# Keeping half of a hidden layer and computing the other half twice: a graph layer with a mixture of experts on one Trainium2 core

## Chip, cores and metric

One core of a Trainium2 chip runs the whole program. The metric is the device time of one execution, in microseconds. All times are of single launches; the profile is of one further launch.

## What is computed

The reference takes node features `x` (6250 nodes, 256 channels), normalizes them, runs two graph convolutions with batch norms over 100,000 edges and adds the result to `x`. Then comes the part that matters here, a feed-forward layer with 8 experts and top-1 routing:

```python
xf = layernorm(x)                                   # 6250 x 256
H = gelu(xf @ W1 + b1)                              # 6250 x 1024
probs = softmax(H @ Wg + bg); assign = argmax(probs)
for e in range(8):
    y = H @ Wd[e] + bd[e]                           # 6250 x 256
    out += where(assign == e, probs[:, e] * y, 0)
return x + out
```

Only the expert that `assign` names counts for a node, so the kernel sorts the nodes by expert and multiplies each tile of 128 sorted nodes with one expert's `Wd`.

## The kernel before

Activations and weights are split in two float16 halves, a high and a low one, and a product is made of three matmuls: high x high, low weight x high, high weight x low. The hidden layer has 1024 units, that is `KH` = 8 chunks of 128. Nodes are taken in tiles of 128 and pairs of tiles of 256. All five engines run one instruction list each, ordered by semaphores; nothing is scheduled automatically. A `Block` ends when all engines have come to its end.

The stages are: `prepare`, the first `aggregate`, `linear1`, `linear2`, the second `aggregate`, `finish_gnn`, and then the two that the change touches.

*The gate stage* (`gate`, 25 pairs in the order of the nodes). GpSimd copies the rows of a pair to `stage`; TensorE transposes them with four fp32 matmuls into bank `TBANK` (`pe_transpose`, L1873); ScalarE (`act_xt`, L1896) and VectorE (`dve_xt`, L1928) make the high and low halves `xt_hi`, `xt_lo`. `pe_hidden` then does 8 chunks of 6 matmuls (L1886), 256 columns each, into four PSUM banks in turn. For each chunk ScalarE takes the Gelu into `hf` (L1913) and, for five of eight, scales it to the high half (L1908); VectorE does the other three (`DVE_HIGH`, L1940) and all low halves (L1945). So `h16` holds the halves of all 8 chunks with the hidden units on the partitions. They are used twice. Once by `logits` on TensorE (L2085), which gives 8 gate logits per node; VectorE's `choose` and TensorE's and VectorE's `ranks` and `place` find the expert and the slot of each node in the order by expert, a few pairs behind. And once by the experts, through DRAM: SP waits for all 8 chunks of a pair (L2022), turns `h16` with one crossbar DMA transpose into rows of 2048 halves per node (`turned`, a ring of `HRING` = 6, L2026), and GpSimd scatters these rows by slot to `sorted_h` (L2068) beside the node's own row in `sorted_rows` (L2062). ScalarE's second instruction of each pair waits until the transpose of two pairs before has read its buffer.

Three places of the ring lie where the down weights of experts 5 to 7 belong (`WDRING` = 3). So `load_wd` brings 5 experts' weights at the head of the stage (5 MB) and the last 3 MB after the last transposes have been scattered from those places (L2028 to L2030). At the end VectorE makes a table of which rows and which expert each of 56 sorted tiles has (`tile_row`, `tile_exp`; L2201 to L2232), and the probabilities are stored.

*The expert stage* (`experts`, 28 pairs of sorted tiles, loops unrolled by `RB4` = 4). For each tile SP reads its row number from the table and issues a transpose from `sorted_h` to `ht`, which brings all 16 half-chunks with the hidden units on the partitions (L2277). ScalarE issues the plain load of the tile's rows from `sorted_rows` (L2331) and computes the residual `x1t` (L2336). GpSimd gathers the probabilities (L2299) and scatters the results (L2304). TensorE does 24 matmuls of 256 columns per tile (L2322): 8 chunks x 3, the weight picked by a register that holds the expert. VectorE adds the bias (L2362), multiplies with the probability and adds the residual (L2369). Buffers `ht`, `r`, `outt` are rings of four pairs: the loads of pair i wait for the results of pair i - 4.

A detail for the steps below: `linear1` fills the padding rows of `sorted_rows` and `sorted_h` from zeros by two DMAs, while its matmuls run.

## Time and profile before

| | us |
|---|---|
| three timed runs | 2112.88, 2133.99, 2148.48 |
| their median | 2133.99 |
| profiled execution | 2117.62 |
| its span in the trace | 2115.9 |
| TensorE busy in it | 1544.6 (73%) |
| VectorE / ScalarE / GpSimd busy | 1053.1 / 775.5 / 976.9 |
| mean granted TensorE clock | 0.902 |

The span is what the profiler saw of the engines; the device time lies 1.7 us above it. All rows below are of this one execution, and their times are us from the start of the span. The busy time of TensorE is an average over stages of different kinds, and an engine's idle time costs something only where it is the one that the others wait for.

### The profile page before, as it was taken

To read this page: it belongs to the slowest core of one execution; us is meant where nothing else is said; L and a number is where in the kernel's file an instruction comes from. 1 tells how busy PE (TensorE), PEld (TensorE's weight loads), DVE (VectorE), ACT (ScalarE), POOL (GpSimd) and SP (SyncE) were. 2 spreads that over 40 slices of the span, in tenths; PEclk is the share of its full clock that TensorE was granted. 3 is DMA by queue.
4 is the path that set the end of the run, shared out by engine and by line. 5 is a ranking of instruction groups with operands and counts; after the bars stand their busy time and mean duration, and the time that the engine had idled before them with its cause. 6 is when DMAs were issued, how large, how long until landed. Compare 5 with 4: busy or idle time off the path is not lost. (4 is left out here: it accounts for less than half of the span.)

```text
span 2115.9 us, 32396 instructions
## 1 busy us (share of the span) xinstructions
PE 1544.6 (73%) x9699; PEld 1063.0 (50%) x9700; DVE 1053.1 (50%) x4210; ACT 775.5 (37%) x1609; POOL 976.9 (46%) x1040
## 2 busy tenths in 40 slices
PE   0123988877888888798688988889767877347885
PEld 0111555544555458686354545455556666235554
DVE  5453766655666635695022333333568677612221
ACT  0451534333443434485123432221476666201010
POOL 5536166665666610002666666663123344424443
PEclk9997999998999999899799999999989898678888
DMA  8324355454545523026677878785578788978884
GB/s 257 103 93 160 117 169 176 155 172 134 178 156 168 172 94 110 10 75 215 204 257 236 310 267 277 270 290 197 178 222 203 199 223 222 267 164 201 193 190 94
DMA packets 378716, 390.36 MB, mean 184 GB/s; under 512 B 245113, under 2 KB 326875, under 8 KB 370798
## 3 DMA queue, kind: packets, MB, share of 16 engines
q1 hardware_dynamic: 314674, 243.69, 38.8%
q0 software_dynamic: 49520, 131.51, 19.3%
q10 hardware_dynamic: 14412, 13.83, 2.4%
q8 instruction: 53, 0.87, 0.2%
q14 instruction: 57, 0.47, 0.1%
HBM read 212.02 MB, written 129.34 MB: 161 GB/s over the span
## 5 line engine op out<-in xcount | busy, mean ns | idle before, releaser
L1166 POOL DMA_INDIRECT grows<-table_dram,gsrc x680 | 654.0, 962 | 529.1 <-issue 290.1
L1100 PE MATMUL ps<-table,adj 128*128 128x512 f16 x2842 | 744.0, 394 | 25.8 <-issue 19.4
L1100 PEld LDWEIGHTS ps<-table,adj 128*128 128x128 f16 x2842 | 393.5, 143 | 216.3 <-issue 66.7
L857 ACT ACTIVATE adj<-ps 128x490 f16<-128x490 f32 (+1 forms) x390 | 215.0, 577 | 317.2 <-PE ps L842 181.5
L828 DVE TENSOR_SCALAR oh_r<-iota_r,keyrem 128x128 f16<-128x128 f16 x780 | 208.7, 269 | 185.1 <-remote 103.2
L842 PE MATMUL ps<-oh_k,oh_r 128*128 128x245 f16 x780 | 154.3, 282 | 120.4 <-issue 51.3
L2322 PE MATMUL ps<-wd,h_sorted 128*128 x1344 | 180.5, 292 | 73.3 <-issue 64.7
L829 DVE TENSOR_SCALAR oh_k<-iota_k,keyrem 128x246 f16<-128x246 f16 x780 | 233.6, 303 | 0.0
L2322 PEld LDWEIGHTS ps<-wd,h_sorted 128*128 128x128 f16 x1344 | 134.6, 104 | 119.2 <-issue 95.3
L842 PEld LDWEIGHTS ps<-oh_k,oh_r 128*128 128x128 f16 x780 | 73.8, 100 | 216.4 <-issue 100.0
L1049 PE MATMUL ps<-grows,oh_g 128*128 128x512 f16 x680 | 175.8, 394 | 4.4 <-issue 2.4
L1886 PE MATMUL ps<-xt_hi,fw_parts 128*128 128x256 f16 (+1 forms) x800 | 132.3, 292 | 17.6 <-issue 12.4
L1913 ACT ACTIVATE hf<-ps,b1f,unscale 128x256 f32<-128x256 f32 (+1 forms) x200 | 110.5, 560 | 87.2 <-PE ps L1886 49.5
L2362 DVE SCALAR_TENSOR_TENSOR y<-ps,inv_g,bdB 128x256 f32<-128x256 f32 x56 | 26.8, 483 | 204.1 <-DMA dst_i<-dst 92.2
L914 DVE TENSOR_SCALAR oh_g<-iota_r,gloc 128x128 f16<-128x128 f16 x680 | 123.1, 272 | 0.3 <-DVE beta L1805 0.2
L921 DVE SCALAR_TENSOR_TENSOR tmp_d<-ps,disP,tmp_d 128x256 f32<-128x256 f32 x30 | 14.5, 483 | 218.1 <-issue 119.2
L1945 DVE SCALAR_TENSOR_TENSOR h<-hf,beta,h 128x256 f16<-128x256 f32 (+1 forms) x200 | 93.0, 493 | 54.9 <-ACT h L1908 51.4
L1133 ACT ACTIVATE agg<-ps 128x256 f32<-128x256 f32 x98 | 37.6, 383 | 216.6 <-remote 166.1
L1049 PEld LDWEIGHTS ps<-grows,oh_g 128*128 128x128 f16 x680 | 68.7, 101 | 83.7 <-issue 14.4
L2336 ACT ACTIVATE x_rows<-in_rows 128x256 f32<-128x256 f32 x56 | 29.2, 589 | 221.1 <-issue 213.6
L2062 POOL DMA_INDIRECT sorted_rows<-rows,slot x49 | 48.8, 997 | 129.7 <-DVE slot L2183 120.9
L2304 POOL DMA_INDIRECT out<-out_rows,out_index x56 | 56.9, 1017 | 103.5 <-DVE out_rows L2369 91.5
(362 smaller groups left out, 2160.1 us busy)
## 6 DMA issues: line engine op xcount, KB each, us to landing
adj_dram<-adj SPq DMA_DIRECT2D x30, 1568.0 KB
adj<-adj_dram SPq DMA_DIRECT2D x30, 1568.0 KB
cv_raw<-fwd SPq DMA_DIRECT2D x64, 256.0 KB
table_dram<-table SPq DMA_DIRECT2D x14, 896.0 KB, 4.1
grows<-table_dram,gsrc POOLq DMA_INDIRECT x680
wd_dram<-cv_parts SPq DMA_DIRECT2D x32, 256.0 KB
in_rows<-sorted_rows ACTq DMA_DIRECT2D x56, 129.5 KB
edge_rows<-packed SPq DMA_DIRECT2D x1, 6392.0 KB
```

The costliest lines, as they stand in the source:

```text
L828: dve.tensor_scalar(a.oh_r[:, n % OHR, i, :], m.iota_r[:, :], m.keyrem[:, 1, j, w:w + 1], None, ALU.is_equal)
L829: last = dve.tensor_scalar(a.oh_k[:, n % OHR, i, :], m.iota_k[:, :], m.keyrem[:, 0, j, w:w + 1], None, ALU.is_equal)
L842: last = pe.matmul(m.ps[:, n % 3, at:at + keys], a.oh_r[:, n % OHR, i, :], a.oh_k[:, n % OHR, i, 0:keys], start=True, stop=True)
L857: act.activation(m.adj[:, q % 3, d0:d0 + wide, :].rearrange("r d c -> r (d c)"), m.ps[:, n % 3, 0:wide * NT], ACT.Copy).then_inc(a.s_adj, 1)
L914: last = dve.tensor_scalar(m.oh_g[:, n % GOR, j, :], m.iota_r[:, :], m.gloc[:, g, part * BT + j:part * BT + j + 1], None, ALU.is_equal)
L1049: last = pe.matmul(acc, m.oh_g[:, n % GOR, j, :], m.grows[:, n % GR, j, :], start=False, stop=part == PT - 1 and j == PARTS[part] - 1)
L1100: last = pe.matmul(acc, adj[:, :, c], table[:, c, :], start=c == 0, stop=c == NT - 1)
L1166: pool.indirect_dma_start(m.grows[:, n % GR, j, :], None, m.table_dram, bass.IndirectOffsetOnAxis(ap=m.gsrc[:, g, part * BT + j:part * BT ...
L1886: last = pe.matmul(m.ps[:, h % UB, 0:n], m.w1[:, 2 * k + half, w, at:at + P], x[:, par, k, 0:n], start=q == 0 and k == 0, stop=q == 2 and ...
L1913: act.activation(m.hf[:, h, 0:n], m.ps[:, h % UB, 0:n], ACT.Gelu, bias=m.b1f[:, h:h + 1], scale=m.unscale[:, 0:1]).then_inc(u.gelu, 1)
L1945: dve.scalar_tensor_tensor(half_of(m, par, 1, h, n), by_tile(m.hf[:, h, 0:n]), m.beta[:, h:h + 1], half_of(m, par, 0, h, n), ALU.mult, ALU ...
L2322: last = pe.matmul(m.ps[:, 2 * (q % 2) + j, 0:C], ht[:, q, j, h, :], w[part], start=z == 0 and k == 0, stop=z == 2 and k == KH - 1)
```

## The change

Of the 8 chunks of the hidden layer, the first `KEPT` = 4 are kept for the experts as before; the other 4 are not stored. The experts compute them a second time from the sorted rows.

- Gate: `h16` becomes `kept` (4 chunks) and `left` (4 chunks). SP's transpose turns `kept` alone, rows are 1024 halves long, and SP waits only until the first 4 chunks of the pair are split. The logits use both. The ring of `turned` is half as large and lies outside the down weights, so all 8 MB of them are loaded at the head of the stage, in four DMAs.
- Experts: `ht` holds 8 half-chunks per tile. `pe_hidden`, `act_hidden` and `dve_hidden`, which now take their list of chunks from `u.chunks`, run for chunks 4 to 7 of each pair (`m.again`), fed by TensorE transposes of `r`. TensorE does pair i's up-projection, in its middle the transposes of pair i + 1, and then the down-projection of pair i - 1. One chunk's high half is VectorE's, three are ScalarE's. The down-projection has its own two banks. SP now issues the loads of `r` too, each behind the transpose of the same tile. VectorE waits for the bias rows before its first work.
- The padding rows of `sorted_h` are half as long.

The core of the diff; edits that only rename or pass on the list of chunks are left out:

```diff
-    m.h16 = take("h16", [P, 2, 2, 2, KH, P], F16)
+    m.kept = take("h_kept", [P, 2, 2, 2, KEPT, P], F16)
+    m.left = take("h_left", [P, 2, 2, 2, KH - KEPT, P], F16)
     assert take.next <= m.ring_at
-    places = [m.ring_at] + [m.wd_at + 8192 * e for e in range(NEXP - WDRING, NEXP)] + [m.ring_at + 8192, m.ring_at + 16384]
-    m.turned = [m.at(f"turned{q}", at, [P, 2, 2 * HID], F16) for q, at in enumerate(places)]
-    assert len(places) == HRING and m.ring_at + 24576 <= m.r5 + 2 * WJ * WP * 4
-    m.hidden = hidden_semaphores(m, "hid")
+    take = Place(m, m.ring_at)
+    m.turned = [take(f"turned{q}", [P, 2, 2 * KEPT * P], F16) for q in range(HRING)]
+    assert take.next <= m.r5 + 2 * WJ * WP * 4
+    m.hidden, m.again = hidden_semaphores(m, "hid", range(KH), (1, 4, 6)), hidden_semaphores(m, "rep", range(KEPT, KH), (1,))
...
+KEPT = 4
+HRING = 6
...
-            load_wd(sp, m, 0, NEXP - WDRING)
+            for e in range(0, NEXP, 2):
+                load_wd(sp, m, e, e + 2)
             for i in range(NPAIR + 1):
                 q, par = i % HRING, i % 2
-                sp.wait_ge(u.split, KH * (i + 2))
+                sp.wait_ge(u.split, KH * (i + 1) + KEPT)
                 if i >= HRING:
                     sp.wait_ge(s_sent[q], 32 * (i // HRING))
                 n = tiles(i)
                 sp.dma_start_transpose(m.turned[q][:, 0:n, :].rearrange("t j (k h) -> t (j k) h", h=P),
-                                       m.h16[:, par, 0:n, :, :, :].rearrange("p j n k t -> p (j n k t)")).then_inc(u.turned[par], 16)
-            for q in range(1, 1 + WDRING):
-                sp.wait_ge(s_sent[q], 16 * sum(tiles(i) for i in range(q, NPAIR + 1, HRING)))
-            load_wd(sp, m, NEXP - WDRING, NEXP)
+                                       m.kept[:, par, 0:n, :, :, :].rearrange("p j n k t -> p (j n k t)")).then_inc(m.s_turned[par], 16)
...
-    take = Place(m, m.ff_at)
-    ht = take("h_sorted", [P, RB4, 2, 2 * KH, P], F16)
-    assert take.next <= m.ring_at
+    take = Place(m, m.ring_at)
+    ht = take("h_sorted", [P, RB4, 2, 2 * KEPT, P], F16)
+    assert take.next <= m.r5 + 2 * WJ * WP * 4
+    u = m.again
...
                     sp.dma_start_transpose(ht[:, q, j, :, :], m.sorted_h[bass.ds(at, P), :]).then_inc(s_ht[q], 16)
+                    sp.dma_start(r[:, q, j, :], m.sorted_rows[bass.ds(at, P), :]).then_inc(s_row[q], 16)
...
+            def transpose(i, par, q, uses):
+                pe.wait_ge(s_row[q], uses)
+                pe_transpose(pe, m, u, i, lambda j, k: r[:, q, j, k * P:(k + 1) * P], 2)
+
+            def down(pe, i, par, q, uses):
+                pe.wait_ge(s_ht[q], uses)
+                for j in range(2):
+                    e = pe.value_load(m.tile_exp[0:1, bass.ds(2 * i + j, 1)], min_val=0, max_val=NEXP - 1)
+                    if j == 0:
+                        pe.wait_ge(u.split, len(u.chunks) * i + 2 * len(u.chunks))
+                    pe.wait_ge(s_y, 2 * i + (j + 1))
+                    for k in range(KH):
+                        w_hi, w_lo = (m.wd[:, bass.ds(e, 1), k // 2, part, k % 2, :].rearrange("p a c -> p (a c)") for part in range(2))
+                        h_hi, h_lo = (ht[:, q, j, part * KEPT + k, :] if k < KEPT else m.left[:, par, j, part, k - KEPT, :] for part in range(2))
+                        for z, (h, w) in enumerate(((h_hi, w_hi), (h_hi, w_lo), (h_lo, w_hi))):
+                            last = pe.matmul(m.ps[:, DB + j, 0:C], h, w, start=z == 0 and k == 0, stop=z == 2 and k == KH - 1)
+                last.then_inc(u.done, 1)
+
+            def step(i, q, k):
+
+                par = q % 2
+                pe_hidden(pe, m, u, i, par, 2, {1: lambda: transpose(i + 1, 1 - par, (q + 1) % RB4, k * 32 + 32 * (1 + (q + 1) // RB4))})
+                down(pe, i - 1, 1 - par, q - 1, k * 32 + 32)
+
+            pe_ahead(pe, u)
+            transpose(0, 0, 0, 32)
+            pe_hidden(pe, m, u, 0, 0, 2, {1: lambda: transpose(1, 1, 1, 32)})
+            pe.wait_ge(m.s_wd, 16 * NEXP // 2)
+            with pe.Fori(0, (NPAIR - 2) // RB4) as k:
+                for q in range(1, RB4 + 1):
+                    step(k * RB4 + q, q, k)
+            last = (NPAIR - 2) // RB4
+            for q in range(1, NPAIR - 1 - last * RB4):
+                step(last * RB4 + q, q, last)
+            pe_hidden(pe, m, u, NPAIR - 1, 1, 2, {})
...
+            act.sem_inc(u.gelu, UB)
+            act_xt(act, m, u, 0, 0, 2)
+            act_hidden(act, m, u, 0, 0, 2, 2)
+            residual(0, 0)
+            with act.Fori(0, (NPAIR - 4) // RB4) as k:
+                for q in range(1, RB4 + 1):
+                    act_hidden(act, m, u, RB4 * k + q, q % 2, 2, 2)
+                    residual(k + q // RB4, q % RB4)
...
+                dve.wait_ge(u.done, i + 3)
                 for j in range(2):
-                    dve.wait_ge(s_down, 2 * i + (j + 1))
-                    dve.scalar_tensor_tensor(y[:, q % 2, j, :], m.ps[:, 2 * (q % 2) + j, 0:C], m.inv_g[:, 0:1],
+                    dve.scalar_tensor_tensor(y[:, q % 2, j, :], m.ps[:, DB + j, 0:C], m.inv_g[:, 0:1],
                                              bd[:, bass.ds(e[j], 1), :].rearrange("p a c -> p (a c)"), ALU.mult, ALU.add).then_inc(s_y, 1)
...
+            dve_xt(dve, m, u, 0, 0, 2)
+            dve_hidden(dve, m, u, 0, 0, 2, 2)
+            for q in range(1, RB4 + 1):
+                dve_hidden(dve, m, u, q, q % 2, 2, 2)
+                results(q - 1, 0, q - 1)
+            with dve.Fori(1, NPAIR // RB4 - 1) as k:
+                for q in range(1, RB4 + 1):
+                    dve_hidden(dve, m, u, RB4 * k + q, q % 2, 2, 2)
+                    dve.wait_ge(s_st[q - 1], 32 * k)
+                    results(RB4 * k + (q - 1), k, q - 1)
```

## Rows read from the trace of the kernel before

**Rows 1.** The page's part 2, 40 equal slices: granted TensorE clock in tenths.

```profile
...
PEclk9997999998999999899799999999989898678888
...
```

**Rows 2.** Chain of waits, last 600 us, summed by line.

```profile
...
by line: PE ps L2322 27.1%; issue 7.2%; SPq L2277 1.6%; DMA h_sorted<-sorted_h 1.0%; another core or an unknown queue 0.8%; SPq L2276 0.3%; DVE y L2362 0.3%; POOL out L2304 0.2%; DVEq L2359 0.1%; DVEq L2271 0.1%; SPq L2280 0.1%; DVE out_row
...
```

**Rows 3.** Busy time by stage: length, engines (instructions), clock, DMA share, GB/s.

```profile
...
810.00:870.00 60.00, 60.00 (x516) 60.00 (x515) 43.90 (x108) 33.35 (x64) 0.00 (x0) 1.00 0.12 47
1563.00:1828.00 265.00, 198.94 (x2193) 165.26 (x2193) 187.04 (x621) 169.29 (x351) 100.03 (x110) 0.89 0.86 221
...
1848.00:1857.00 9.00, 0.00 (x0) 0.00 (x0) 0.00 (x0) 0.00 (x0) 0.00 (x0) 0.50 0.15 53
1857.00:1865.00 8.00, 0.00 (x0) 0.00 (x0) 0.00 (x0) 0.00 (x0) 0.00 (x0) 0.50 0.00 0
...
1875.00:2103.00 228.00, 180.50 (x1344) 134.61 (x1344) 50.91 (x140) 28.18 (x55) 107.31 (x109) 0.88 0.86 184
...
```

**Rows 4.** The same view in stretches of the expert stage.

```profile
...
1915.00:1934.00 19.00, 18.32 (x139) 14.67 (x140) 5.07 (x15) 0.00 (x0) 7.01 (x8) 0.86 0.84 194
1934.00:1942.00 8.00, 3.65 (x20) 1.49 (x19) 0.42 (x2) 0.00 (x0) 4.91 (x5) 0.72 1.03 219
...
2092.00:2095.00 3.00, 1.58 (x12) 1.02 (x13) 0.82 (x2) 0.00 (x0) 0.34 (x1) 1.00 0.01 1
...
```

**Rows 5.** Chain of waits near the end: start, us, what.

```profile
...
2083.90 2.81 PE ps L2322 x24
...
2086.81 2.82 PE ps L2322 x24
...
```

**Rows 6.** Busy time by stretch, gate stage.

```profile
...
1698.00:1767.00 69.00, 50.88 (x614) 42.85 (x612) 52.66 (x177) 46.91 (x98) 31.18 (x34) 0.99 0.88 225
...
1745.00:1748.00 3.00, 0.64 (x9) 0.26 (x5) 2.53 (x10) 1.43 (x3) 2.50 (x3) 1.00 0.95 308
...
```

**Rows 7.** Three source lines: count, ns min/median/max, first and last start.

```profile
...
L2026 SPq DMA_TRANSPOSE turned<-h x25: 4771/4842/5892, 1575.1 to 1819.8; - x25
...
L2277 SPq DMA_TRANSPOSE h_sorted<-sorted_h x56: 168/2234/5085, 1865.8 to 2079.4; - x56
...
L2331 ACTq DMA_DIRECT2D in_rows<-sorted_rows x56: 6/344/746, 1865.9 to 2077.4; - x56
...
```

**Rows 8.** Instructions in order of time, gate: start us, us, what.

```profile
...
1759.42 0.60 PE L1873 MATMUL ps<-id,stage 128*128 128x128 f32 x4
...
1759.86 0.60 PE L1886 MATMUL ps<-xt_hi,fw_parts 128*128 128x256 f16 x4
...
1760.52 0.60 PE L1886 MATMUL ps<-xt_hi,fw_parts 128*128 128x256 f16 x4
...
```

**Rows 9.** Source line 2322, same columns.

```profile
...
L2322 PE MATMUL ps<-wd,h_sorted x1344: 268/273/422, 1875.1 to 2100.3; 128*128 x192
L2322 PEldq FUSED_REGOPS  x896: 2/46/1055, 1875.0 to 2099.5; - x180
...
```

**Rows 10.** Groups of instructions from 1500 us: busy us, mean ns, idle before.

```profile
...
L1913 ACT ACTIVATE hf<-ps,b1f,unscale 128x256 f32<-128x256 f32 (+1 forms) x200 | 110.5, 560 | 87.2 <-PE ps L1886 49.5 <-remote 21.8 <-issue 5.7
L1945 DVE SCALAR_TENSOR_TENSOR h<-hf,beta,h 128x256 f16<-128x256 f32 (+1 forms) x200 | 93.0, 493 | 54.9 <-ACT h L1908 51.4 <-issue 0.7
...
L1908 ACT ACTIVATE h<-hf,beta 128x256 f16<-128x256 f32 (+1 forms) x125 | 62.4, 499 | 0.8
...
L2336 ACT ACTIVATE x_rows<-in_rows 128x256 f32<-128x256 f32 x56 | 29.2, 589 | 221.1 <-issue 213.6 <-DMA in_rows<-sorted_rows 7.4
...
L2362 DVE SCALAR_TENSOR_TENSOR y<-ps,inv_g,bdB 128x256 f32<-128x256 f32 x56 | 26.8, 483 | 204.1 <-DMA dst_i<-dst 92.2 <-PE ps L2322 63.3 <-issue 48.6
...
L1928 DVE TENSOR_TENSOR xt_lo<-ps,xt_hi 128x512 f16<-128x512 f32 (+1 forms) x25 | 16.8, 673 | 3.5 <-ACT xt_hi L1896 3.5
...
```

**Rows 11.** Chain of waits at the experts' start: start, us, what.

```profile
...
1868.33 0.29 SPq L2276
...
```

**Rows 12.** GpSimd in order of time, end of the gate block.

```profile
...
1842.80 1.55 POOL L2068 DMA_INDIRECT sorted_h<-turned,slot  x1 [0.30 <-DMA sorted_h<-turned,slot]
...
```

More of the change, by code:

```diff
@@ L1853, in hidden_semaphores @@
     u.done = m.sem(f"{tag}_done")
-    u.turned = [m.sem(f"{tag}_turned{q}") for q in range(2)]
     return u
 def pe_ahead(pe, u):
-    pe.sem_inc(u.up, 2 * KH)
+    pe.sem_inc(u.up, 2 * len(u.chunks))
     pe.sem_inc(u.done, 2)
@@ L1864, in dve_ahead @@
     dve.sem_inc(u.xt, 1)
-    dve.sem_inc(u.split, KH)
+    dve.sem_inc(u.split, len(u.chunks))
 def pe_transpose(pe, m, u, i, rows, ntile):
@@ L1877, in pe_hidden @@
 def pe_hidden(pe, m, u, i, par, ntile, between):
-    n = ntile * P
+    n, each = ntile * P, len(u.chunks)
     pe.wait_ge(u.xt, i + 2)
-    for h in range(KH):
-        pe.wait_ge(u.gelu, i * KH + (h + 1))
-        half, at = divmod(h * P, 512)
+    for at, h in enumerate(u.chunks):
+        pe.wait_ge(u.gelu, i * each + (at + 1))
+        half, c = divmod(h * P, 512)
         for q, (w, x) in enumerate(((0, m.xt_hi), (1, m.xt_hi), (0, m.xt_lo))):
             for k in range(KC):
-                last = pe.matmul(m.ps[:, h % UB, 0:n], m.w1[:, 2 * k + half, w, at:at + P], x[:, par, k, 0:n],
+                last = pe.matmul(m.ps[:, at % UB, 0:n], m.w1[:, 2 * k + half, w, c:c + P], x[:, par, k, 0:n],
@@ L1906, in high @@
             return
-        act.wait_ge(u.gelu, i * KH + (h + 1 + UB))
+        act.wait_ge(u.gelu, i * each + (at + 1 + UB))
         act.activation(half_of(m, par, 0, h, n), by_tile(m.hf[:, h, 0:n]), ACT.Copy, scale=m.beta[:, h:h + 1]).then_inc(u.hi, 1)
-    for h in range(KH):
-        act.wait_ge(u.up, i * KH + (h + 1 + 2 * KH))
-        act.wait_ge(u.split, i * KH + (h + 1))
-        act.activation(m.hf[:, h, 0:n], m.ps[:, h % UB, 0:n], ACT.Gelu, bias=m.b1f[:, h:h + 1],
+    for at, h in enumerate(u.chunks):
+        act.wait_ge(u.up, i * each + (at + 1 + 2 * each))
+        act.wait_ge(u.split, i * each + (at + 1))
+        act.activation(m.hf[:, h, 0:n], m.ps[:, at % UB, 0:n], ACT.Gelu, bias=m.b1f[:, h:h + 1],
@@ L1914, in act_hidden @@
                        scale=m.unscale[:, 0:1]).then_inc(u.gelu, 1)
-        if h == 0:
+        if at == 0:
             act.wait_ge(u.done, i + 1)
-            if n_turned is not None:
-                act.wait_ge(u.turned[par], n_turned)
-        else:
-            high(h - 1)
-        if h == 3 and nxt:
+            if turned is not None:
+                act.wait_ge(m.s_turned[par], turned)
+        else:
+            high(at - 1, h - 1)
+        if at == min(3, each - 2) and nxt:
             act_xt(act, m, u, i + 1, 1 - par, nxt)
-    high(KH - 1)
+    high(at, h)
@@ L1933, in dve_hidden @@
 def dve_hidden(dve, m, u, i, par, ntile, nxt, between={}):
-    n = ntile * P
+    n, each = ntile * P, len(u.chunks)
     highs = 0
-    for h in range(KH):
-        if h in DVE_HIGH:
-            dve.wait_ge(u.gelu, i * KH + (h + 1 + UB))
+    for at, h in enumerate(u.chunks):
+        if at in u.dve_high:
+            dve.wait_ge(u.gelu, i * each + (at + 1 + UB))
             dve.tensor_scalar(half_of(m, par, 0, h, n), by_tile(m.hf[:, h, 0:n]), m.beta[:, h:h + 1], None, ALU.mult).then_inc(u.own, 1)
-            dve.wait_ge(u.own, i * len(DVE_HIGH) + (DVE_HIGH.index(h) + 1))
+            dve.wait_ge(u.own, i * len(u.dve_high) + (u.dve_high.index(at) + 1))
         else:
             highs += 1
-            dve.wait_ge(u.hi, i * (KH - len(DVE_HIGH)) + highs)
+            dve.wait_ge(u.hi, i * (each - len(u.dve_high)) + highs)
         dve.scalar_tensor_tensor(half_of(m, par, 1, h, n), by_tile(m.hf[:, h, 0:n]), m.beta[:, h:h + 1], half_of(m, par, 0, h, n),
                                  ALU.mult, ALU.subtract).then_inc(u.split, 1)
-        if h == 3 and nxt:
+        if at == min(3, each - 2) and nxt:
             dve_xt(dve, m, u, i + 1, 1 - par, nxt)
-        if h in between:
-            between[h]()
+        if at in between:
+            between[at]()
 REG = 6528
@@ L2000, in gate @@
     m.s_prob, m.s_wd = s_store, S("i_wd")
+    m.s_turned = [S(f"i_turned{q}") for q in range(2)]
     s_sent = [S(f"i_sent{q}") for q in range(HRING)]
@@ L2326, in _ @@
+            last = (NPAIR - 2) // RB4
+            for q in range(1, NPAIR - 1 - last * RB4):
+                step(last * RB4 + q, q, last)
+            pe_hidden(pe, m, u, NPAIR - 1, 1, 2, {})
+            for i in range(NPAIR - 2, NPAIR):
+                down(pe, i, i % 2, i % RB4, 32 * (i // RB4) + 32)
         @block.scalar
         def _(act):
[L2328 to L2331 removed]
```

85 lines of the change are left out of this document (31 added, 54 removed).

## The prediction

> **What bounds the kernel now.** I read the page first, then the chain, then the stages. The page's slices show TensorE's granted clock at 0.6 to 0.9 in the last eighth, below most of what comes before [rows 1]. The chain of work that ended last, asked for the final 600 us, runs through the down-projection matmuls (L2322) and through "issue", time in which TensorE waited for nothing that the profile shows [rows 2]. The change touches the last two stages, so I cut the span there [rows 3]: the gate stage, in which every activation is computed, takes about 265 us (1563 to 1828); then comes a pause of 47 us, in which the token-to-expert table is made, the scatters drain and the block ends; the expert stage has its matmuls from 1875 to 2100.6, 225.7 us, or 8.06 us for each of its 28 pairs of tiles.
>
> The expert stage alternates [rows 4]. It runs some 18 us in which matmuls come steadily (139 in 19 us), then 6 to 8 us in which only 20 come, and the clock falls to its lower level (granted 0.72 in that stretch, a mixture of 1.2 and 2.4 GHz). In a steady stretch at 2.4 GHz one tile of 24 matmuls takes 2.81 us and the next begins 2.91 after it began [rows 5], so a pair is 5.8 us of work. The other 2.24 us of the 8.06 are pauses and the half clock behind them. The gate stage does the same once per pair: its pair takes 10.1 us in the long stretch at full clock (1698 to 1767), and some 3 us of each are a hole in TensorE like 1745 to 1748 [rows 6]. No semaphore explains these holes. DMA is 0.86 busy in both stages [rows 3], and SP issues crossbar transposes through both [rows 7]; that they are the cause is not shown.
>
> **The change, part by part.**
>
> *Up-projection again, in the experts.* Per pair TensorE gets 4 chunks x 6 = 24 matmuls of 256 columns. Four of them take 0.44 us from start to start, and a chunk of six 0.66 us, [rows 8]: 4 x 0.66 = 2.64 us. The four fp32 transposes of the rows take 0.44 us [rows 8]. The 48 down matmuls stay. TensorE's work at full clock is 5.82 + 2.64 + 0.44 = 8.9 us a pair.
>
> *Pauses.* This is the unknown term. Instructions of a pair now: 48 matmuls, 48 weight loads, 32 register operations (896 for 28 pairs), [rows 9], and by the code 10 of value loads and waits: 138. After: 28 more of each of the first two and some 6 waits, 200. Lower bound: the pauses go away, since half of the transposes' traffic does: 8.9 us. Upper bound: they keep their present price per instruction, 2.24 us for 138: 3.25 us for 200, and the pair takes 12.1 us. Between them lies the rate at which TensorE took instructions: matmuls plus loads, (614 + 612) / 69 = 17.8 per us in the gate [rows 6], 138 / 8.06 = 17.1 in the experts; at 18 per us 200 instructions are 11.1 us. After the last SP transposes, with DMA down to 0.01, one hole was 3 us instead of 6 to 8 [rows 4], so I expect some relief and take 10.6 us a pair.
>
> *The other engines in the experts.* ScalarE gets 4 Gelu (0.56), 3 copies (0.50), one xt copy (at most VectorE's 0.67 for the same operand) beside 2 residuals (0.59): 2.24 + 1.5 + 0.67 + 1.18 = 5.6 us [rows 10]. VectorE gets 4 x 0.48 for the low halves (the 0.49 of the group), at most 0.50 for one copy and 0.67 for xt, beside four results of 0.48: 5.0 us, with gaps and value loads under 7 [rows 10]. Both stay under 8.9, so I cost them at nothing; the cover is TensorE's own 8.9 us, and were it gone they would bind near 7. GpSimd's four indirect DMAs do not change.
>
> *SP's queue.* It has two transposes a pair, 2.23 us each in the median [rows 7], and gets the two row loads of ScalarE's queue (0.34 us) behind each transpose, with the value load (0.29) and register work about 0.7 us per tile [rows 11]. At unchanged transpose time that is 2 x (2.23 + 0.34 + 0.7) = 6.5 us, under 8.9; at half, 4.3. What waits behind it: the rows of pair i wait for the outputs of pair i - 4, and TensorE's transposes of pair i, which sit ahead of the down matmuls of pair i - 2, wait for these rows. The loop of four pairs is 2.5 up-projections and 3 down-projections (2.5 x 3.1 + 3 x 5.8 = 25.2 us), results 2.2, SP 6.5 and, as an estimate, 3.5 for the landing: 37.4 us, 9.4 us a pair. Under 10.6, so nothing; it would be a floor if the pauses went.
>
> *Start of the experts.* First matmul now at 1875.1 [rows 9], 10.2 us after the block starts (1864.9: nothing runs until 1865, [rows 3]). After, VectorE waits for the bias rows before anything, and it must make xt before the up-projection starts: rows by about +6, bias rows by about +11, xt 1.5: first up-projection at +12.5 (bounds +8 and +16). Then 28 x 10.6 = 296.8. Expert stage: 309.3 against 235.7, +73.6 us. Bounds by the pair: 8.9 gives +26, 12.1 gives +115.6.
>
> *Gap between the stages.* The late load of 3 MB of down weights (L2030) goes, and the scattered rows of activations halve. GpSimd's last scatter is issued at 1842.8 [rows 12], DMA still moves in the stretch up to 1857, and then 8 us pass with nothing at all [rows 3]. I take the tail of the scatters away but keep the 8 us and the table on VectorE, which has nothing to do after 1848: -8.5 us, bounds 0 and -10.
>
> *Gate stage.* The arithmetic is the same; its transposes take SP 4.84 us each [rows 7] and may take half. By DMA alone nothing is gained, since TensorE's hole does not wait for a transfer. If the holes come from the transposes, up to 1.3 us a pair are to be had before VectorE binds (busy 52.7 of 69 us [rows 6], 7.7 of 10.1 a pair; the small gaps between its 26 instructions take it to perhaps 8.8, an estimate): 23 x 1.3 = 30. If not, zero. The 8 MB of weights are now loaded at once at its head (3 MB more, 14 us at the stage's 221 GB/s, beside the first transposes, for which the third pair waits): 0 to +5. I take -8 for the stage, bounds -30 and +5. The halved padding transfer in linear1 lies beside 60 us of full TensorE work [rows 3]: nothing.
>
> *Sum.* +73.6 - 8.5 - 8 = +57. The profiled execution took 2117.62 us (span 2115.9): 2175 on its own scale. It lies 16 us under the median of the three timed runs, 2133.99, which spread from 2112.88 to 2148.48; set on that median, the forecast is 2191.
>
> **Two rules of the skill that bear on the pauses.** In the trace the clock is at 1.2 GHz only beside the holes. The Trainium skill, TensorE: Matmul & The Clock Gate, Part 1, says that the gate's default is the throttled level and that activity releases it; by it a denser stream would hold 2.4 GHz. The trace agrees for the stretch from 1698 to 1767, granted 0.99 [rows 6]. The Trainium skill, Runtime: NRT & Kernel Launch, Instruction fetch mechanics, says that TensorE's instruction memory holds 2048 instructions and that fetch is hidden; by it a price per instruction should not exist. The rows with holes speak against it, but the stage with 516 matmuls in 60 us has none at 17.2 instructions per us [rows 3], so the rule can't be thrown out. Both lead to the first rival.
>
> **Rivals.**
>
> R1, not slower: the pauses are caused by the transposes' traffic, and with half the packets in a longer stage they go. The place is TensorE's stream; the price is 2.24 us a pair in the experts and about 1.1 in the gate; it decides once a pair falls under 10.1 us. Experts +26 to +40 (8.9, or 9.4 with the ring of rows), gap -8.5, gate -25: -7.5 to +6.5, about 2134 on the median. For it: linear1 without holes at light DMA, and the short hole when DMA was quiet. Against: a hole of 3 us stood where DMA was at 0.01 [rows 4].
>
> R2: the pauses go by instructions. 12.1 us a pair: +115.6 - 8.5 + 0 = +107, 2241. For it: the gate and the experts have nearly the same rate, 17.8 and 17.1, with different work. Against: the same DMA load in both.
>
> R3: SP's longer queue binds: transposes of half the size still take 2.2 us and the rows queue behind them, rows landing 8 us late instead of 3.5. Then the loop of four is 41.9 us, or 10.5 a pair, and a stall in TensorE is added to remaining pauses: 11.4 a pair, +96 - 16.5 = +80, 2214.
>
> **How the numbers follow.** Forecast (partial relief, 10.2 to 11.2 a pair, +44 to +76): 0.50. R1: 0.28. R2: 0.16. R3: 0.06. A measurement of this kernel can tell about 2%, 43 us: under 2091 is faster, over 2177 slower. Slower: nearly all of the forecast, R2 and R3: 0.67. Same: R1 but for a tail, and the forecast's low edge: 0.29. Faster: 0.04, if the gate stage also gained from ScalarE's and VectorE's gaps. The range leaves out a tenth on either side: from R1's middle, 2131, to just over R2, 2245.
>
> **What would show it.** The expert stage: up matmuls beside L2322 and a pair of about 10.6 us; no late weight load; nothing between the table's end and the 8 us of silence; gate pairs near 9.8 us; holes in TensorE still there in both stages, shorter. Wrong: if the stage has no holes (R1), if pauses per instruction are the same (R2), if TensorE's transposes wait for in_rows (R3), or if ScalarE or VectorE, whose dependent steps I took as hidden, hold TensorE up in every pair.

## The result and the profile after

The changed kernel takes 2170.72 us, the median of four runs (2165.66 to 2176.45), against 2130.94 (2112.88 to 2148.48) for the kernel before in the same session: +39.8 us, where the forecast was 2191 and +57. The ratio is 1.0208, with a 95% interval of 1.0158 to 1.0257, when the one slow execution of the kernel before, 2148.48, is left out. The interval holds the 2% that the prediction took as what can be told; that the changed kernel is slower at all is clear. The profiled execution took 2176.45 us, its span 2174.4.

First the page's slices of the granted clock, then the chain of waits over the last 594 us, which answer to [rows 1, 2]. Stretches of a view that are left out are marked by three dots:

```profile
PEclk9997989999999899898899899999988997599998
...
```

```profile
by line: PE ps L2332 25.6%; PE ps L1889 12.6%; issue 3.7%; PE ps L1876 2.0%; DMA bdB<-fbd 1.0%; SPq L2282 0.4%; POOL out L2310 0.2%; DVE xt_lo L1932 0.2%; SPq L2281 0.2%; DVE y L2388 0.2%; SPq L2283 0.2%; ACT xt_hi L1900 0.1%; DVE h_left L1
```

The last five slices, 0.7 and 0.8 in [rows 1], are 0.9 now but for the very last, which is mostly the tail. The chain runs through TensorE's own work, the down matmuls (L2332) and the second up-projection (L1889), and "issue" fell from 7.2% to 3.7%. The stages, in the columns of [rows 3] (gate; table and scatters; wait for the block's end; start of the experts; their matmuls; tail):

```profile
1580.00:1848.00 268.00, 205.72 (x2192) 171.24 (x2192) 185.77 (x617) 168.89 (x351) 98.90 (x109) 0.85 0.54 139
1848.00:1870.00 22.00, 1.79 (x11) 1.11 (x11) 16.52 (x67) 0.53 (x1) 12.26 (x11) 0.50 0.30 103
1870.00:1884.00 14.00, 0.00 (x0) 0.00 (x0) 0.21 (x1) 0.00 (x0) 0.00 (x0) 0.50 0.05 15
1884.00:1896.00 12.00, 1.12 (x4) 0.72 (x4) 0.47 (x1) 1.88 (x2) 1.98 (x2) 0.50 0.70 182
1896.00:2158.00 262.00, 239.78 (x2120) 207.50 (x2121) 122.52 (x303) 133.74 (x279) 109.43 (x108) 0.99 0.47 105
2158.00:2174.00 16.00, 0.67 (x7) 0.36 (x4) 1.74 (x5) 0.00 (x0) 1.97 (x2) 0.63 0.00 0
```

Cut at the same events in both traces (first up matmul of the gate, last logits, first instruction of SP's expert block, first and last expert matmul):

| us | before | after | difference | forecast |
|---|---|---|---|---|
| start to first up matmul of the gate | 1563.4 | 1580.4 | +17.0 | 0 |
| gate stage | 262.4 | 267.2 | +4.8 | -8 |
| logits' end to the experts' block | 39.0 | 36.5 | -2.5 | -8.5 |
| experts: start | 10.1 | 12.2 | +2.1 | +2.3 |
| experts: matmuls | 225.2 | 262.1 | +36.9 | +71.3 |
| tail | 15.6 | 16.0 | +0.4 | 0 |

The first line is not the change. Nothing ahead of the gate differs but the size of one hidden padding transfer. Two later profiles of the two kernels on one chip had it at 1302.5 and 1304.6, and on another chip the changed kernel and its variants spread from 1569 to 1590. Without it the rows add up to +41.7, near the +39.8 of the medians. So nearly all of the loss is in the experts' matmuls: 9.36 us a pair for 8.04.

TensorE in order of time over one pair of the changed kernel (start us, us, what, idle before):

```profile
1939.69 0.61 PE L1889 MATMUL ps<-xt_hi,fw_parts 128*128 128x256 f16 x4
...
1941.01 0.60 PE L1876 MATMUL ps<-id,in_rows 128*128 128x128 f32 x4
...
1942.76 1.47 PE L2332 MATMUL ps<-wd,h_sorted 128*128 x12
1944.07 1.47 PE L2332 MATMUL ps<-wd,h_left 128*128 x12
1945.38 1.47 PE L2332 MATMUL ps<-wd,h_sorted 128*128 x12
1946.69 0.93 PE L2332 MATMUL ps<-wd,h_left 128*128 x7
1948.43 0.70 PE L2332 MATMUL ps<-wd,h_left 128*128 x5 [0.81 <-issue]
1948.97 0.60 PE L1889 MATMUL ps<-xt_hi,fw_parts 128*128 128x256 f16 x4
```

From the first up matmul to the first down matmul are 3.07 us (24 up matmuls and four transposes, forecast 2.64 + 0.44). The 48 down matmuls come at 1.31 us a dozen, 5.24 us (forecast 5.82). The pair takes 9.28, so 0.97 us are pause, in one place near the end of the down matmuls, where the forecast had 1.7. The pauses of the stage are the idle time of TensorE that its rows put down to "issue", that is, to nothing that the trace shows (us, times, longest; the kernel before, then the changed one):

```profile
PE ps L2322 <- issue: 64.7, 55, 28.4
...
PE ps L2332 <- issue: 18.0, 29, 0.9
```

The longest of the first row, 28.4 us, lies ahead of the stage's first matmul, so the pauses fell from 36.3 to 18.0 us. The half clock behind them, which the kernel before paid for in [rows 4], is gone: granted 0.99.

Three source lines, the columns of [rows 7], and the last scatter of GpSimd, beside [rows 12]:

```profile
L2032 SPq DMA_TRANSPOSE turned<-h_kept x25: 1286/2702/12232, 1588.8 to 1839.6; - x25
L2282 SPq DMA_TRANSPOSE h_sorted<-sorted_h x56: 842/1257/1901, 1884.9 to 2132.1; - x56
L2283 SPq DMA_DIRECT2D in_rows<-sorted_rows x56: 5/436/706, 1886.4 to 2133.9; - x56
...
1865.99 1.56 POOL L2071 DMA_INDIRECT sorted_h<-turned,slot  x1 [0.30 <-issue]
```

Halving the chunks halves what SP spends on a transpose, 2.23 to 1.26 us and 4.84 to 2.70. The last scatter is issued 18.4 us after the last logits, where it was 17.0; from its issue to the experts' block it is 18.1 us for 22.1. The halved transfers save 4.0 us there, and GpSimd's issue of a scatter takes as long as before (1.56 us for 1.55).

### The profile page after: what moved, and what is told of

Read it like the earlier page. It is cut to its first block and busy times, and to the rows that moved or that the text cites. A ratio compares the mean times of both kernels' runs of the same rounds, so it can differ in the third digit from the quotient of the medians.

```text
span 2174.4 us, 34707 instructions
## 1 busy us (share of the span) xinstructions
PE 1620.4 (75%) x10483; PEld 1145.4 (53%) x10484; DVE 1128.0 (52%) x4378; ACT 882.4 (41%) x1833; POOL 979.9 (45%) x1040
## 5 line engine op out<-in xcount | busy, mean ns | idle before, releaser
L857 ACT ACTIVATE adj<-ps 128x490 f16<-128x490 f32 (+1 forms) x390 | 215.2, 576 | 324.8 <-PE ps L842 193.4
L1917 ACT ACTIVATE hf<-ps,b1f,unscale 128x256 f32<-128x256 f32 (+1 forms) x312 | 173.5, 561 | 213.0 <-PE ps L1889 167.7
L1889 PE MATMUL ps<-xt_hi,fw_parts 128*128 128x256 f16 (+1 forms) x1248 | 206.1, 292 | 27.5 <-ACT hf L1917 13.4
L1889 PEld LDWEIGHTS ps<-xt_hi,fw_parts 128*128 128x128 f16 x1248 | 126.6, 105 | 54.4 <-issue 21.7
L1889 PE MATMUL ps<-xt_lo,fw_parts 128*128 128x256 f16 (+1 forms) x624 | 128.6, 291 | 1.2 <-issue 1.2
L1949 DVE SCALAR_TENSOR_TENSOR h_left<-hf,beta,h_left 128x256 f16<-128x256 f32 (+1 forms) x212 | 99.6, 489 | 45.1 <-ACT h_left L1912 36.1
L1125 ACT ACTIVATE tmp_d<-ps,disP 128x256 f32<-128x256 f32 x30 | 14.2, 473 | 236.5 <-remote 173.9
L2332 PE MATMUL ps<-wd,h_left 128*128 x672 | 87.9, 272 | 18.4 <-issue 18.0
```

The source lines that it names most:

```text
L857: act.activation(m.adj[:, q % 3, d0:d0 + wide, :].rearrange("r d c -> r (d c)"), m.ps[:, n % 3, 0:wide * NT], ACT.Copy).then_inc(a.s_adj, 1)
L1889: last = pe.matmul(m.ps[:, at % UB, 0:n], m.w1[:, 2 * k + half, w, c:c + P], x[:, par, k, 0:n], start=q == 0 and k == 0, stop=q == 2 and k ...
L1917: act.activation(m.hf[:, h, 0:n], m.ps[:, at % UB, 0:n], ACT.Gelu, bias=m.b1f[:, h:h + 1], scale=m.unscale[:, 0:1]).then_inc(u.gelu, 1)
L1949: dve.scalar_tensor_tensor(half_of(m, par, 1, h, n), by_tile(m.hf[:, h, 0:n]), m.beta[:, h:h + 1], half_of(m, par, 0, h, n), ALU.mult, ALU ...
L2332: last = pe.matmul(m.ps[:, DB + j, 0:C], h, w, start=z == 0 and k == 0, stop=z == 2 and k == KH - 1)
```

## The experiments

Eight of the kernels below ran on two other chips, on which the kernel before takes 1802 and 1805 us; the last four on one where it takes 2123. The whole program differs by that much, not only the stages in question, so a number is compared only with those of its own kind. The chip of 1802 has no profile of either kernel: its four kernels are read against the two profiles of the chip of 1805. The times of these four, and on the last chip those of the changed kernel, of its rows put first and of the product left out, are of one execution each. The expectations of the first four were worked out from the first session's stages (8.04 and 9.36 us a pair), so they are read as differences. "us a pair" is the time of the experts' matmuls over 28.

**The two kernels again, on a chip with hardly a pause.**

> The kernel before, for its trace beside the next three on the same chip. The four runs so far came from a chip on which the kernel before takes 1802 us and TensorE's pauses are nearly absent even at the old traffic. Theory C (the pauses belong to the chip, not to the kernel): either the chip is of that kind, pauses under 10 us in the expert stage and 7.1 to 7.5 us a pair, the DMA share then being the bound, or it is of the slower kind, 8.0 us a pair with some 33 us of pauses, total 2110 to 2150. Theory D again would need pauses in proportion to the traffic on either kind.

> The change. Theory C on a chip without pauses: 8.9 to 9.1 us a pair (TensorE's work), expert stage about 264 us, gate 220 us against 232, total about 1840, ratio 1.02. On a chip with pauses as in the first result: 9.36 us a pair, gate 267 us, ratio 1.02.

1805.38 us and 1834.37 (1831.98 to 1837.81), ratio 1.0164 [1.0132, 1.0196]. Busy time of the kernel before (gate, then experts), then of the changed one:

```profile
1302.00:1535.00 233.00, 181.59 (x2187) 155.34 (x2188) 186.10 (x615) 167.14 (x351) 98.12 (x106) 0.92 0.96 243
1589.00:1784.00 195.00, 163.06 (x1343) 130.09 (x1344) 49.80 (x136) 26.68 (x53) 105.80 (x107) 0.96 0.99 215
...
1610.00:1750.00 140.00, 115.44 (x956) 92.21 (x955) 36.54 (x100) 20.55 (x40) 80.64 (x82) 0.96 1.02 230
```

```profile
1304.00:1523.00 219.00, 176.31 (x2178) 152.76 (x2179) 184.43 (x614) 169.99 (x351) 97.97 (x106) 0.94 0.70 169
...
1572.00:1818.00 246.00, 237.91 (x2123) 208.10 (x2124) 122.33 (x303) 133.86 (x279) 109.09 (x108) 0.99 0.50 112
```

A pair is 6.96 us before and 8.78 after, each a little under what was expected (7.1 to 7.5, and 8.9 to 9.1). Before, SP is the bound: from 1580 to 1780 its queue never waits for a result, and its two transposes a pair (2.49 us each in the median) with their value loads and register work fill the pair. In the first session it waited 11 times for one, 16.0 us. The DMA share is 0.99 to 1.02 beside it, where it was 0.86 in [rows 3]; how much of the 2.49 us comes from that, no run here separates. After, the share is 0.50, and TensorE runs a pair without any gap, up matmul to up matmul 8.46 us:

```profile
1700.67 0.60 PE L1889 MATMUL ps<-xt_hi,fw_parts 128*128 128x256 f16 x4
...
1703.89 1.47 PE L2332 MATMUL ps<-wd,h_sorted 128*128 x12
1705.20 1.47 PE L2332 MATMUL ps<-wd,h_left 128*128 x12
1706.51 1.47 PE L2332 MATMUL ps<-wd,h_sorted 128*128 x12
1707.82 1.47 PE L2332 MATMUL ps<-wd,h_left 128*128 x12
1709.13 0.60 PE L1889 MATMUL ps<-xt_hi,fw_parts 128*128 128x256 f16 x4
```

Another row that differs with the pauses is that of the register operations which make the addresses of the down weights. They take 46 ns in the median everywhere, but the longest took 1055 ns in [rows 9] and 729 in the changed kernel of the first session, and 51 and 46 here (the kernel before here, then the changed one in the first session and here):

```profile
L2322 PEldq FUSED_REGOPS  x896: 46/46/51, 1589.1 to 1783.3; - x180
...
L2332 PEldq FUSED_REGOPS  x896: 4/46/729, 1905.6 to 2157.7; - x180
...
L2332 PEldq FUSED_REGOPS  x896: 46/46/46, 1582.0 to 1817.4; - x180
```

In the experts of the first session 33 (before) and 31 (after) of TensorE's register operations took 0.3 us or more, 22.9 and 21.2 us in all, and all but three of the 64 carry no wait. So part of a pause is TensorE's own queue standing in an operation that needs no other engine.

The experts lose 52.4 us here (206.2 to 258.6), but the gate stage gains 13.8 (232.6 to 218.8) and the gap 6.7. The gate's gain has its row in who waited for the transposes of the gate, before and after:

```profile
  ACT hf L1913: 25.9, 10
...
```

```profile
  ACT hf L1917: 5.3, 1
...
```

TensorE itself has no pauses in the gate here. It stands mostly before `place`, for VectorE's `slot`: 45.8 us (21 times) before and 35.6 (21 times) after, in the first session 7.2 and 4.6. In the first session the kernel before had 2.6 us of ScalarE's wait for a transpose, and TensorE's pauses were 50.6 us in the gate. That these made the pairs long enough for a transpose of 4.84 us to be in time is argued from the two traces, not tested.

**Half of each transpose in the kernel before.** The low halves are not fetched, and the high ones stand in for them, so this kernel's output lacks the low parts.

```diff
-sp.dma_start_transpose(ht[:, q, j, :, :], m.sorted_h[bass.ds(at, P), :])
+sp.dma_start_transpose(ht[:, q, j, 0:KH, :], m.sorted_h[bass.ds(at, P), 0:HID])
-... ht[:, q, j, h, :], w[part],
+... ht[:, q, j, h % KH, :], w[part],
```

> The kernel before, with the experts' transposes cut to the first 8 of 16 half-chunks (half the crossbar traffic); the down matmuls read these 8 twice, so TensorE's instructions are as before and the low halves of the activations are left out of the sum. Theory D (TensorE's pauses in the experts come from the transposes' DMA traffic): pauses go, a pair takes 5.8 to 6.3 us, the expert stage (block start to last down matmul) about 175 to 190 us against 235.7. Theory N (they come from TensorE running through its instructions faster than about 22 per us, whatever the DMA does): 8.0 us a pair and 235 us as before, the clusters of pauses every 25 us still there.

1775.08 us; 6.16 us a pair, for 6.96:

```profile
1590.00:1758.00 168.00, 155.74 (x1323) 125.21 (x1320) 49.80 (x136) 26.97 (x52) 105.24 (x106) 0.99 0.75 161
```

This is the change's gain without its price: 0.8 us a pair from halving the transposes on this kind of chip. TensorE is then busy 155.7 of 168 us, and SP waits for results again:

```profile
SPq L2276 <- DVE out_rows L2369: 41.5, 23, 2.1
```

The change adds 3.07 us of TensorE work to get it. The edit halves the transfers and SP's time on them at once, so it doesn't tell the two apart. The 6.16 us lie in theory D's range, but the kernel before has next to no pauses here (4.9 us), so this says nothing on their cause.

**Twice the transposes in the changed kernel.**

```diff
 sp.dma_start_transpose(ht[:, q, j, :, :], m.sorted_h[bass.ds(at, P), :]).then_inc(s_ht[q], 16)
+again = more[:, q, j, :, :] if q < 2 else m.kept[:, q - 2, j, :, :, :]...
+sp.dma_start_transpose(again, m.sorted_h[bass.ds(at, P), :]).then_inc(s_ht[q], 16)
```

> The kernel after, with each of the experts' transposes issued twice, the second into a place that nobody reads: the crossbar traffic per pair is that of the kernel before. Theory D: the pauses come back, a pair takes 11 us or more instead of 9.36, the stage over 315 us against 274.4. Theory N: within 3 us of 274, since SP's queue (two more issues of 1.26 us a pair) is not the bound.

1884.72 us, 10.52 us a pair. What the engines waited for (us, times, longest):

```profile
PEld ps L1876 <- DMA in_rows<-sorted_rows: 40.8, 16, 4.2
PE ps L1876 <- DMA in_rows<-sorted_rows: 35.8, 15, 4.0
```

TensorE waits for the rows, which now stand behind four transposes on SP. That is rival R3's mechanism, near the 10.5 us that the prediction worked out for its loop of four pairs (its forecast was 11.4, with pauses on top). TensorE has no pause by the row of "issue", so twice the transposes (DMA share 0.70 for 0.50) didn't bring them on this chip. Neither theory's expectation fits: the traffic brought no pauses, and SP's queue did become the bound.

**More instructions.** 32 matmuls of 16 columns, with their weight loads, behind each pair's down matmuls, into a bank that nobody reads.

```diff
+for k in range(32):
+    last = pe.matmul(m.ps[:, 7, 0:16], ht[:, q, 0, k % 8, :], m.wd[:, 0, 0, 0, 0, 0:16], ...)
 last.then_inc(u.done, 1)
```

> The kernel after, with 32 more matmuls of 16 columns (64 more instructions) behind each pair's down-projection, into an unused bank. They cost about 1.1 us of work a pair. Theory D: 9.36 + 1.1 = 10.5 us a pair, stage about 306 us, no clusters. Theory N: the buffer of instructions runs dry as in the gate, whose burst is the same: another 2 to 3 us a pair, 12.5 to 13.5 us, stage 360 us or more.

1854.0 us, 9.39 us a pair for 8.78:

```profile
1575.00:1836.00 261.00, 256.53 (x3003) 231.07 (x3003) 122.19 (x302) 133.17 (x278) 109.90 (x108) 0.99 0.47 104
```

64 instructions cost 0.61 us, 10 ns each; the kernel before's pauses over its instructions, R2's price, would be 2.24 / 138, or 16 ns, 1.04 us. TensorE has no pause in the stage by the row of "issue". On this chip there is no pause by instruction count, and both theories' numbers were too high: 64 instructions more cost less than the 1.1 us of work that they were given.

**The rows on SP, in the kernel before.**

```diff
 sp.dma_start_transpose(ht[...], ...).then_inc(s_ht[q], 16)
+sp.dma_start(r[:, q, j, :], m.sorted_rows[bass.ds(at, P), :]).then_inc(s_row[q], 16)
-act.wait_ge(s_out, k * RB4 + (q + 1 - RB4 + 2))
-load(k * RB4 + q, q)
```

> The kernel before, with the row loads of the experts moved from ScalarE's queue to SP's, each behind its tile's transpose, as the change does. Theories D and N: no difference in the pauses, stage 232 to 242 us. Theory Q (two queues that issue at the same time cause TensorE's pauses): pauses shrink, stage under 215 us. If SP's longer queue is the bound here (two transposes of 2.2 us and two loads are 6.5 us a pair against 8.06), stage over 245.

1825.21 us, 7.68 us a pair for 6.96. Waits of the stage:

```profile
ACT x_rows L2337 <- DMA in_rows<-sorted_rows: 226.9, 28, 48.2
...
POOL prob_rows L2300 <- DMA in_rows<-sorted_rows: 112.8, 27, 35.3
```

Moving the loads was not free where the transposes are long (2.17 us each): 20 us. SP's queue does not wait for a result between 1600 and 1800 here either, while the DMA share of the stage is 0.83 for 0.99. So it is the length of SP's queue, and not a full DMA, that sets the pair here, and the row loads add to it. No run moved the loads back in the changed kernel; there SP waits 22 times for results, 67.6 us between 1600 and 1790, so its queue has room.

**The weights' load spread out.**

```diff
-for e in range(0, NEXP, 2):
-    load_wd(sp, m, e, e + 2)
+load_wd(sp, m, 0, 2)
 ... # behind the transpose of pair i:
+if i in (6, 10, 14):
+    load_wd(sp, m, (i - 2) // 2, (i - 2) // 2 + 2)
```

> The change with its four loads of down weights spread over the gate stage (at the head and behind the transposes of pairs 6, 10 and 14) instead of all at the head. If the loads at the head hold back the first transposes (ScalarE waited 5.4 us for one after the change), gate 4 to 7 us shorter than after; if not, within 1 us.

1829.83 us (1827.14 to 1831.13), ratio 1.0136 [1.0107, 1.0165], 4.5 us under the changed kernel of the same chip; its gate stage takes 215.2 us for 218.8, 3.6 us less and just under the 4 to 7 expected. The load of all weights at the head costs about 4 us, inside the 0 to +5 of the forecast.

**Six chunks kept.** The last two experts' weights are loaded late, and the up-projection's four banks are used in turn.

```diff
-KEPT = 4
+KEPT = 6
+WDRING = 2
-m.ps[:, at % UB, 0:n]
+m.ps[:, (par * each + at) % UB, 0:n]
```

> Six chunks kept and two computed again, with the weights of the last two experts loaded late as before. If TensorE's work is the bound of the expert stage after the change, a pair is 2 x 0.66 us shorter than after: 7.6 to 8.1 us, the expert stage 37 us shorter, total 25 to 37 us under after, which is about the kernel before (ratio 0.99 to 1.01). If the ring of rows or ScalarE's and VectorE's steps bind, it is shorter by less than 20 us.

1844.82 us (1839.52 to 1857.14), ratio 1.0209 [1.0179, 1.0239]: slower than with four kept, 9.55 us a pair. Less work on TensorE, and a longer stage. Its waits:

```profile
ACT xt_hi L1901 <- PE ps L1877: 55.2, 27, 4.2
...
PE ps L1877 <- DMA in_rows<-sorted_rows: 32.8, 13, 3.0
```

The rows of a pair are late, and with only two chunks to compute TensorE has less in front of it when they are. The waits (32.8 us inside the loop; the 60 us named in an expectation below include 27.4 us ahead of the first matmul) are not all of it: the granted clock of the stage is 0.88 for 0.99, so matmuls at the lower clock stand behind them. Both ends of the expectation missed; it had the stage shorter either way. The kernels of the next part try that.

**Six kept, with the rows ahead of the transposes; and four kept so.** The changed kernel ran again beside them, for its stages on this chip.

```diff
-for j in range(2):
-    at = sp.value_load(...); transpose(j); row(j)
+at = [sp.value_load(...) for j in range(2)]
+for j in range(2): row(j)
+for j in range(2): transpose(j)
```

> The changed kernel unaltered, as the one that the other three runs of this call are read against on their own chip. Both theories (the experts are bound by TensorE's work; the experts are bound by something that TensorE waits for) expect 8.7 to 9.4 us a pair, as in the two profiles of it so far (8.78 on a chip with nearly no pauses of TensorE, 9.36 on one with 23 us of them), and a total within 1.3 to 2.1% over the kernel before of the same chip.

> The changed kernel with both row loads of a pair issued ahead of its two transposes on SP, instead of each behind one. At four kept chunks TensorE's work bounds the pair, so under the first theory it stays at 8.7 to 8.9 us a pair (on a chip without pauses) and the total within 6 us of the changed kernel; the first pair's transposes of x can start 1.3 us earlier, which is the one sure gain. If the late rows cost the changed kernel something in the loop too, the pair falls by up to 0.3 us, 8 us in all.

> Six chunks kept and two computed again, and both row loads of a pair issued ahead of its two transposes. With six kept TensorE's work is 5.82 + 1.32 + 0.44 = 7.6 us a pair, yet the run with the rows behind the transposes took 9.55, with TensorE waiting 60 us for the rows. If what held it was the way from a pair's result over SP's queue to the rows of the pair four later (the rows waited behind one to two transposes of 1.44 us), it falls to 7.6 to 8.2 us a pair: 1.4 to 1.9 us x 28 are 38 to 55 us less than with the rows behind, which is 0 to 1% over the kernel before where that kernel has 6.96 a pair, and level with it or faster where it has 8.04. If the transposes themselves (their transfer, not their place in the queue) or the short chain of only two chunks hold it, it stays over 9 us a pair and 2% over the kernel before.

The kernel before took 2123.46 us here, the changed one 2190.43 (9.52 a pair, 19.4 us of pauses, the gate's first matmul at 1590.4). That is one execution, 3.2% over the kernel before and outside both the 8.7 to 9.4 us and the 1.3 to 2.1% expected. Four kept, rows first: 2163.48, one execution too, with the gate's first matmul at 1572.0: 18.4 of the 27 us between the two lie ahead of the stages in question. It has 9.23 a pair with 12.8 us of pauses. The 6.6 us fewer pauses are most of the 8.1 us (0.29 a pair), so little or nothing is left for the order of the queue. Six kept, rows first: 2161.1 (2154.18 to 2169.27), ratio 1.0168 [1.0101, 1.0234], 8.92 a pair. The wait for rows inside the loop is gone, another took its place (the waits, then TensorE and VectorE in order of time):

```profile
PE ps L2336 <- DVE y L2392: 37.1, 26, 1.7
DVE y L2392 <- remote: 124.2, 25, 5.4
...
2005.88 0.82 PE L2336 MATMUL ps<-wd,h_left 128*128 x6
...
2009.18 0.88 DVE L2392 SCALAR_TENSOR_TENSOR y<-ps,inv_g,bdB 128x256 f32<-128x256 f32 x2 [5.01 <-remote]
...
2009.92 0.28 PE L2336 MATMUL ps<-wd,h_sorted 128*128 x1 [1.47 <-DVE y L2392]
```

26 times TensorE stands 1.4 us before the down matmuls until VectorE has read the last pair's product. The second computation of two chunks and the transposes, 1.75 us, would cover that reading of 0.88 us, were it prompt. But VectorE starts only 2.5 us after the last down matmul (2006.70 to 2009.18); in the changed kernel it was 0.15 us (1949.13 to 1949.28). The trace dates TensorE's step of `u.done`, for which VectorE waits, at 2009.05. Over the stage this step comes 2.27 us after the end of its matmul in the median, and 0.01 us in the changed kernel on the same chip; hence "remote". The ends of matmuls are modelled, so the trace can't tell whether the matmuls ended later or the signal came late, and no run settles why.

**One product less in the second computation.** The product with the low half of x is left out of chunks 4 to 7 in the experts.

```diff
+terms = (...)[:3 if u is m.hidden else 2]
-for q, (w, x) in enumerate(((0, m.xt_hi), (1, m.xt_hi), (0, m.xt_lo))):
+for q, (w, x) in enumerate(terms):
```

> The second computation of chunks 4 to 7 leaves out the product with the low half of x (two of its six matmuls a chunk), so its result is less precise; eight matmuls of 256 columns a pair go, and nothing else. If TensorE's own work bounds the experts, as I hold, all of the removed time comes out: 8 x 256 columns at 2.4 GHz are 0.85 us a pair, so about 7.9 us a pair where the changed kernel has 8.78, 24 us less in all. If the queue of SP and the ring of four rows bind it, the pair stays at 8.5 us or more, under 8 us less in all. If the chain from TensorE over the gelu, the split and back binds, it is between the two, since the chunk's chain gets only its matmul time shorter.

2163.17 us (one execution; the gate's first matmul at 1569.2), 9.23 a pair for 9.52: 0.29 less, where 0.85 had been expected. The wait for rows in the loop, in this kernel and, over its whole span, in the changed one of the same chip (where 21.8 of 22.8 us are the first):

```profile
PE ps L1876 <- DMA in_rows<-sorted_rows: 19.9, 21, 3.3
```

```profile
PE ps L1876 <- DMA in_rows<-sorted_rows: 22.8, 3, 21.8
```

So only a third came out, while waits for the rows of 19.9 / 28 = 0.71 us a pair appeared. The rest does not add up to it simply: the pauses fell from 19.4 to 6.5 us, the granted clock from 0.99 to 0.96, and the step of `u.done` comes 1.15 us late in the median, as in the run above, which would make the ring's loop longer. The changed kernel is bound by TensorE, but on this chip the ring of four rows stands close below it.

## Why the prediction was right, and where it was not

The direction and the place were right: TensorE's second computation costs more than the halved transposes give, the chain goes through L2332 and L1889, and nothing of the other engines holds it. The forecast of 2191 missed 2170.72 by 20 us, and less than its terms, since errors cancelled, which is luck: in the profiles' stages the experts came out 34.6 us under the forecast, the gate 12.8 over, the gap 6.0 over. By the prediction's own line for slower, 2177, to which it gave 0.67, the median lies 6 us on the side of "same".

- *TensorE's work, 8.9 us a pair.* The up-projection and the transposes took 3.07 for 3.08. The down matmuls took 5.24 for 5.82: the 2.91 us of [rows 5] from tile to tile held a value load and a wait beside the 2.62 us of 24 matmuls. Work 8.3; the pair shown on a chip without pauses took 8.46.
- *Pauses: the term that was mis-sized.* "At 18 per us 200 instructions are 11.1 us", and from it 10.6 a pair. The measured 9.36 lies below all of the 10.2 to 11.2 that the forecast stood for. TensorE took its 200 instructions in 9.36 us here, 21 per us, and in 8.78 elsewhere. The rate of [rows 3, 6] was a result of the pauses and not a limit, as more instructions at 28 per us (264 in 9.39) then showed. What the pair holds beyond the work of 8.31 is 1.05 us, not 1.7; 0.64 of it are pauses by the row of "issue" (18.0 / 28). Together with the shorter down matmuls this is the 1.24 us x 28 = 34.7 us of the experts.
- *Start, +12.5 after the block starts.* Measured 12.2.
- *Gap, -8.5.* Measured -2.5, on the other chip -6.7. From the last scatter's issue to the block 4.0 us were saved, but the scatter was issued 1.4 us later.
- *Gate, -8.* Measured +4.8, on the other chip -13.8. Its pauses fell from 50.6 to 40.2 us, but TensorE's waits for ScalarE's Gelu rose from 1.2 us (2 times) to 13.4 (10 times) and the granted clock fell from 0.89 to 0.85, for which no run here shows a cause. The wait for a transpose that the change removes was only 2.6 us there.
- *The rings and queues (at no cost).* They cost nothing at four kept chunks, as forecast, but the loop was worked out wrongly: the 9.4 us given as a floor "if the pauses went" is none, since without pauses the pair took 8.78, with 3.9 us of waits for rows in the whole stage. The rows did hold TensorE up with a product less on the last chip (9.23), at six kept and at doubled transposes.

The rivals: R1 gave the pair's size (8.9 to 9.4) better than the forecast did, but the total that it drew from it (2134) needed 25 us from the gate, which weren't there, and its cause does not hold alone. The kernel before ran with more of its DMA time used on the other chip (0.99 for 0.86) and had 4.9 us of pauses in the experts for 36.3. R2's price per instruction fails in the first session already: 200 instructions a pair for 138, and half the pauses. On a chip without pauses more instructions brought none; on one with them no instructions were added. Fewer transposes and fewer pauses came together there, so that halved traffic relieved them, R1's cause, is neither shown nor excluded. R3 is real, at 10.52 us, when the transposes are doubled, and not at their present size.

What stays open is what the pauses are. They come mostly in single gaps of 0.3 to 1.3 us without a releaser, and in register operations of TensorE's queue stretched from 0.05 to as much as 1.05 us, in the first session and on the last chip and hardly on the two others, in the gate and the experts of either kernel. They follow the chip more than the kernel; neither transposes nor the instruction count brought them back where they were absent. The experiments on their cause all ran on a chip without them, and none on one with them. What the change costs depends little on them by the two comparisons with several executions, +40 and +29 us, though a single one gave +67. None of the changed kernel's variants beats the kernel before; the nearest is the changed kernel with its weights' load spread, at 1.0136.

## What to carry to other kernels

Work that is recomputed to save transfers is paid in full on the engine that computes, and gives back only the stretch by which the queue of transfers was longer than that engine's own work: on the chip without pauses 3.07 us a pair were added and the pair grew by 1.82, of which halving the transposes alone gives back 0.8. Ask which queue issues the transfers and whether it ever waits: SP's never did there, and that, more than the DMA share, named the bound. Take an engine's work from back-to-back rows and never from a rate that already holds unexplained pauses. When a stage gets shorter work per step, list the loops over the ring again: at six kept chunks first the rows and then the read of PSUM held TensorE up, and in the first of these less work took longer.

## What the runs showed that was not expected

The kernel before takes 1802 and 1805 us on two chips, 2123 and 2131 in the other two sessions, though the changed kernel's experts have a granted clock of 0.99 in both (over the whole span the kernel before has 0.902 and 0.950, and its gate starts at 1563.4 and 1302.5 us). The Trainium skill, Runtime: NRT & Kernel Launch, Instruction fetch mechanics, has instruction fetch mostly hidden, except behind a taken branch that leaves what is fetched. The trace's branches in the experts are too few for that to be the pauses: 7 and 6 on TensorE in the first session, against 54 and 29 pauses. For the rest the stretch from 1700.67 to 1709.13 on one chip agrees, 200 instructions without a gap, and the pause of 0.81 us that stands in the same place of the same code on another is not accounted for by it, nor by any releaser in the trace.
